# Decoder layer, mixer stage: the acausal half of the decay factors zeroed by GpSimd after the exponential instead of masked by a product before it

## What is computed

```python
def step(carry, inp):
    sr, si, px = carry
    dt_t, A_t, tr_t, th, bt, ct, xt = inp
    alpha = jnp.exp(A_t * dt_t)[:, :, None, None]
    beta = ((1.0 - tr_t) * dt_t)[:, :, None, None] * alpha
    gamma = (tr_t * dt_t)[:, :, None, None]
    base = bt[:, None, None, :] * (px[..., None] * beta + xt[..., None] * gamma)
    ...
    y = ...   # the state read out with ct
```

## Time and profile before

| what | us |
|---|---|
| median of the timed runs (3) | 699.77 (695.93 to 700.83) |
| the profiled execution, its own time | 701.77 |
| its span, first to last instruction | 700.0 |
| PE busy in the span | 610.4 (87%) |
| DVE busy | 495.2 (71%) |
| POOL busy | 261.2 (37%) |
| ACT busy | 256.6 (37%) |

### The profile page before, as it was taken

One profiled execution on the slowest core, in us unless ns is written; L12 is line 12 of the kernel. 1 busy time (PEld: TensorE's weight loads), 2 busy tenths in 40 slices (PEclk: granted clock), 3 DMA queues, 4 the chain that ended last, 5 costly groups with the idle time before them and its releaser, 6 DMA issues. The chain is left out here.

```text
span 700.0 us, 17981 instructions
## 1 busy us (share of the span) xinstructions
PE 610.4 (87%) x6368; PEld 502.8 (72%) x6368; DVE 495.2 (71%) x1246; ACT 256.6 (37%) x444; POOL 261.2 (37%) x301
## 2 busy tenths in 40 slices
PE   6589999999999754888779879779799999999995
PEld 5467778778777553676667767557688888888884
DVE  2877887887887554657567667486578778787873
ACT  2443442443343200635445435335322323332221
POOL 4263754754752575405145144362101101110111
PEclk9989999999999975789999999999999999999998
DMA  6020000000000485275484763800001000000000
GB/s 204 0 62 1 16 15 0 15 15 14 1 16 1 114 200 99 70 142 133 106 159 126 138 132 93 188 6 6 32 0 32 30 0 30 30 0 30 16 16 16
DMA packets 53553, 40.34 MB, mean 58 GB/s; under 512 B 3968, under 2 KB 48288, under 8 KB 53488
## 3 DMA queue, kind: packets, MB, share of 16 engines
q1 hardware_dynamic: 50896, 36.74, 22.2%
q0 software_dynamic: 704, 1.92, 1.2%
q10 hardware_dynamic: 1888, 0.79, 0.6%
HBM read 24.10 MB, written 11.93 MB: 51 GB/s over the span
## 5 line engine op out<-in xcount | busy, mean ns | idle before, releaser
L1917 PE MATMUL bank<-xT_hl_c,w_up 128*128 128x512 f32 x432 | 118.1, 409 | 2.4 <-ACTq L67 2.4
L1244 DVE TENSOR_REDUCE nmax<-bank 128x4 f32<-128x512 f32 x112 | 72.0, 685 | 54.9 <-PE bank L1399 48.3
L141 POOL TENSOR_TENSOR rstd<-mv,norm_c 128x4 f32<-128x4 f32 x24 | 6.4, 267 | 264.3 <-DVE mv L135 251.2
L1151 ACT ACTIVATE prob<-bank 128x512 f32<-128x512 f32 x128 | 69.4, 594 | 67.2 <-PE bank L1399 42.0
L1917 PEld LDWEIGHTS bank<-xT_hl_c,w_up 128*128 128x128 f32 x432 | 76.1, 189 | 15.9 <-ACTq L67 2.7
L1389 PE MATMUL bank<-neg_i,mask 64*128 64x256 bf16 x512 | 54.3, 292 | 36.4 <-issue 9.5
L1839 ACT ACTIVATE sg<-bank 128x512 f32<-128x512 f32 x72 | 43.0, 597 | 105.3 <-PE bank L1917 105.3
L1933 PEld LDWEIGHTS bank<-w_down,hid 128*128 128x128 f32 x576 | 74.4, 191 | 5.9 <-issue 0.5
L738 POOL TENSOR_TENSOR ramp<-upto,dec_hl 128x512 fp32r<-128x512 f32 x64 | 66.8, 1073 | 26.1 <-PE bank L866 26.1
L1933 PE MATMUL bank<-w_down,hid 128*128 128x128 f32 x576 | 75.6, 275 | 0.0
L1872 DVE TENSOR_TENSOR gu<-sg,bank 128x512 f32<-128x512 f32 x64 | 43.8, 685 | 21.5 <-PE bank L1917 10.5
(11 more groups left out here) (227 smaller groups left out, 1265.1 us busy)
## 6 DMA issues: line engine op xcount, KB each, us to landing
q_stack<-q_scratch SPq DMA_DIRECT2D x32, 192.0 KB, 5.4
k_scratch<-k_part SPq DMA_DIRECT2D x8, 384.0 KB, 3.2
q_scratch<-q_part SPq DMA_DIRECT2D x8, 384.0 KB, 2.7
k_stack<-k_scratch SPq DMA_DIRECT2D x32, 96.0 KB
x<-xT_in SPq DMA_DIRECT2D x8, 256.0 KB, 8.3
mask<-mask_in SPq DMA_DIRECT2D x8, 256.0 KB, 6.0
xres<-x_in SPq DMA_DIRECT2D x8, 256.0 KB, 2.8
q_scratch<-q_part SPq DMA_DIRECT2D x8, 256.0 KB, 3.1
```

The lines of the kernel that those rows point to most:

```text
L1151: act.activation(prob[:, b % 2, ORDER[n], :, :], (TT0, TT1)[n % 2][:, :], ACT.Exp, scale=XD ** -0.5)\
L1244: dve.tensor_reduce(nmax[:, b, 4 * u:4 * u + 4], (SS0, SS1)[n % 2][:, :].rearrange("p (i k) -> p i k", i=4), AX_X, ALU.max, negate=True).t ...
L1917: mm = pe.matmul(bank[:, :], w_up[:, which, a, c, :], xT_hl[par][:, v, :], start=(n == 0), stop=(n == 2))
```

## The change

In `front`, the product `ident` x `acausal` is gone, and `acausal` with the two POOL instructions that made it. `expo` now holds finite values in its acausal half after the exponential (all exponents are sums of decays, at most 0). A new POOL helper `causal(g, b)` waits for the exponential, and sets the entries with s > t of `expo` to 0 in place, with one affine selection over 128x512. DVE's `mix` waits for that selection instead of for the exponential. POOL's ramps and selections take turns, one ramp pair and one selection at a time; `steps_of` and `normalise_pool` stay behind them, and in group 7 the three `part_third` are spread among them.

```diff
--- before.py
+++ after.py
@@ -312,7 +312,6 @@
         w_out = t["w_out"]
         upto = sb("upto", [P, P])
         after = sb("after", [P, P], F32R)
-        acausal = sb("acausal", [P, P], BF16)
         phase = sb("phase", [P, 1])
 
         soft = sb("soft", [P, NSEQ, 2 * HEADS])
@@ -348,6 +347,8 @@
         s_xx = sem("x_mm", GS)
         s_g = sem("g_mm", GS)
         s_exp = sem("expo_ready", GS)
+        s_causal = sem("expo_causal", GS)
+        pool_passed = ctx.enter_context(nc.semaphore("mixer_pool_passed"))
         s_w = sem("w_ready", 3 * GS)
         s_mix = sem("mix_ready", GS)
         s_y = sem("y_mm", GS)
@@ -511,11 +512,6 @@
                                    pattern=[[1, P]], channel_multiplier=-1).then_inc(s_pool, 1)
                 for k, value in enumerate((LN_EPS, -0.5)):
                     pool.memset(norm_c[:, k, :], value).then_inc(s_pool, 1)
-                pool.wait_ge(s_pool, 5)
-                pool.memset(scratch[:, :], 0.0).then_inc(s_pool, 1)
-                pool.wait_ge(s_pool, 8)
-                pool.affine_select(out=acausal[:, :], in_=scratch[:, :], compare_op=ALU.is_ge, fill=NEG, base=0,
-                                   pattern=[[1, P]], channel_multiplier=-1).then_inc(s_pool, 1)
                 pool.memset(c_rot[:, :, :, :, :], 0.0).then_inc(s_off, 1)
                 pool.wait_ge(s_dve, DONE[0])
                 steps_of(pool, 0)
@@ -728,7 +724,7 @@
 
         @block.gpsimd
         def _(pool):
-            for s in (s_x1, *a.third):
+            for s in (s_x1, s_causal, *a.third):
                 s.prime(pool)
 
             def ramps(g, bs):
@@ -739,17 +735,34 @@
                                            bc(dec_hl[:, v, bass.ds(g * GS + b, 1), :].rearrange("p o h -> p (o h)")[:, :, None],
                                               [P, HEADS, P]), ALU.mult).then_inc(s_ramp.sem, 1)
 
+            def causal(g, b):
+
+                pool.wait_ge(s_exp.sem, s_exp.at(g, b))
+                pool.sem_inc(pool_passed, 1)
+                pool.affine_select(out=expo[:, b % 2, :, :], in_=expo[:, b % 2, :, :], compare_op=ALU.is_ge, fill=0.0, base=0,
+                                   pattern=[[0, HEADS], [1, P]], channel_multiplier=-1).then_inc(s_causal.sem, 1)
+
             def group(g, par, left):
-                ramps(g, (2, 3))
-                if left:
-                    ramps(g + 1, (0, 1))
+                ramps(g, (2,))
+                causal(g, 1)
+                if not left:
+                    part_third(pool, a, 0, 1)
+                ramps(g, (3,))
+                causal(g, 2)
+                if left:
+                    ramps(g + 1, (0,))
+                else:
+                    part_third(pool, a, 0, 0)
+                causal(g, 3)
+                if left:
+                    ramps(g + 1, (1,))
+                    causal(g + 1, 0)
                 if left == 2:
                     steps_of(pool, g + 2)
                 if left:
                     normalise_pool(pool, g, s_res, s_x1, res, mv, rstd, norm_c, x1[:, bass.ds(g * GS, GS), :])
                 if not left:
-                    for group_, which in ((0, 1), (0, 0), (1, 1)):
-                        part_third(pool, a, group_, which)
+                    part_third(pool, a, 1, 1)
                 if left == 1:
                     pool.memset(a.first[1][:, :, :].bitcast(F32), TWO_ONES).then_inc(a.ones, 1)
 
@@ -757,6 +770,7 @@
             ramps(0, (0, 1))
             betas(pool, 1)
             steps_of(pool, 1)
+            causal(0, 0)
             pairs(pool, group)
 
         @block.vector
@@ -807,7 +821,7 @@
                     if b:
                         inputs_of(g, b)
                     dve.wait_ge(s_g.sem, s_g.at(g, b))
-                    dve.wait_ge(s_exp.sem, s_exp.at(g, b))
+                    dve.wait_ge(s_causal.sem, s_causal.at(g, b))
                     dve.wait_ge(s_y.sem, s_y.at(g, b - 2))
                     dve.tensor_tensor(mix[:, b % 2, :, :], PG[:, :].rearrange("p (h t) -> p h t", h=HEADS),
                                       expo[:, b % 2, :, :], ALU.mult).then_inc(s_mix.sem, 1)
@@ -862,9 +876,8 @@
                 pe.wait_ge(s_ramp.sem, s_ramp.at(g, 2 * b + 1))
                 pe.wait_ge(s_exp.sem, s_exp.at(g, b - 1))
                 for v in range(2):
-                    pe.matmul(PD[:, :], after[:, :], ramp[:, b % 2, v, :, :], start=(v == 0), stop=False)
-                pe.matmul(PD[:, :], ident[:, :], bc(acausal[:, None, :], [P, HEADS, P]), start=False, stop=True)\
-                    .then_inc(s_dec.sem, 1)
+                    mm = pe.matmul(PD[:, :], after[:, :], ramp[:, b % 2, v, :, :], start=(v == 0), stop=(v == 1))
+                mm.then_inc(s_dec.sem, 1)
                 pe.wait_ge(s_w.sem, s_w.at(g, 3 * b - 2))
                 tokens(par, b, 0)
```

## The result

The changed kernel took 709.29 us (median of 4 runs, 708.48 to 713.90), the kernel before 700.30 us (4 runs). The ratio is 1.0144, with a 95% interval of 1.0086 to 1.0202. Over all runs of the study the medians are 709.2 us (7 runs) and 700.2 us (37). One run of the changed kernel, 719.5 us, was in a slower state of the chip and is left out. The profiled execution of the changed kernel took 708.48 us, with a span of 706.7.

The account below looks back on a forecast made before the run. PE was taken to bound the mixer, busy 22.25 of 23 us. The terms -6.1, +16.9, -5.2, +1.5 and +7.0 (clock) sum to +14.1 us, on a median of 699.8 us: 713.9 us, range 704 to 720.

Parts of the forecast that it names:

- the second rival: Mixer: PE stalls before theta come, but the clock stays up; 706.9 us, chance 0.26.
- The product that goes: PE in groups 0 to 6: 29 products of ident and acausal fall away at 0.21 us each, -6.1 us.
- The selection: POOL: one 128x512 selection takes 0.67 us, bounds 0.60 and 0.88.
- The stall: Start of groups 1 to 6: PE waits before theta for POOL's late steps, 6 x 2.81 = +16.9 us.
- What the stall covers: Groups 1 to 6: PE's waits for ramps and `mix` vanish behind the stall, -5.2 us; late `rotate` costs nothing.
- The end of the mixer: Group 7: two selections ahead of the third part of q delay SP's stores, +1.5 us.
- The clock: PE behind the stalls: granted clock falls to 0.50 after five of six, 5 x 1.4 = +7.0 us.
- The third: Mixer: DVE becomes late as well, `w_tok` held 0.57 us in each of six groups, +3.4 us; 717.3 us, chance 0.12.
- The fourth rival: Mixer: POOL finishes selection and steps before PE reaches theta, and `rotate` isn't late; 690.0 us, chance 0.06.

Follow-up runs that it names:

- busy_stall: The changed kernel with ten more 128x512 matmuls of PE ahead of each wait for the steps, their result overwritten by theta: 704.6 us.
- product_back: The changed kernel with the product of ident and acausal kept as well: 711.7 us.
- after_again: The changed kernel, unchanged, profiled and measured again: 709.2 us.
- q_part_early: The changed kernel with, in group 7 alone, the third part of q ahead of the selection of sequence 2: 709.4 us.
- two_selections: The changed kernel with the selection of the next group's sequence 0 done twice over: 713.7 us.
- both_early: The changed kernel with POOL's steps and ramps of the next group's sequence 2 ahead of its sequence 0's selection and the normalisation, group 6's memset also earlier: 688.7 us.
- steps_first: The changed kernel with the steps for theta made ahead of the selection of the next group's sequence 0: 701.9 us.

## Why the prediction was right, and which terms were off

The direction, the mechanism and its place were right, and 709.3 us lies in the range. The size was 9 us, not 14. The total alone wouldn't have told the forecast from the second rival, whose 706.9 us lies nearer to 709.3 than 713.9 does; the six stalls and the four falls of the clock in the trace do. Term by term, for the point where the attention begins (12.0 us instead of 14.1):

- **The product that goes**, -6.1 us. Taken out of the kernel before it was worth about 5.2 us (4.23 in six groups, and group 0). The difference is the one product per group that only lengthens a wait for ramps.
- **The selection**, 0.67 us on a line between two sizes: 0.64 us undisturbed, 0.70 us in the mean.
- **The stall**, 6 x 2.81 = 16.9 us: from output to theta 2.61, 2.66, 2.63, 2.64, 2.60 and 2.44 us more than before, 15.6 us. Every link of the chain was there.
- **What the stall covers**, -5.2 us: together with the 24 products of groups 1 to 6 the sum had 10.2 us. Without falls of the clock (busy_stall) theta to output was 9.0 us shorter. The remaining 1.2 us are put down to `rotate` and `mix`, which come late by more than the stall covers: in busy_stall's trace PE's weight loads wait for `rotate` six times, 2.7 us in all. The prediction called that gap "some tenths" and priced it at nothing.
- **The end of the mixer**, +1.5 us: 2.2 us. The part of q ends 1.85 us later after the first ramp, behind two selections of 0.64 and 0.82 us and a ramp pair that took 2.49 us instead of 2.02. Why the second selection and the ramps took longer was not tested.
- **The clock**, 5 x 1.4 = 7.0 us: the term that was most off. It fell four times, at 1.1 us each, 4.4 us. That the fall follows such a stall was right, and theta itself did lose 1.5 us. But PE, when slow, later waits less for `rotate`, and gets some of it back: such waits are two in the changed kernel (1.0 us), six in busy_stall (2.7 us). Where the product keeps PE busier (product_back), the two falls cost 1.65 and 1.39 us (24.19 and 23.93 us from theta to output against 22.54), so there the prediction's 1.4 was right. The rule "nearly as long, so five of six" had no more behind it than one row. Stalls of the same 2.3 to 2.5 us were followed by a fall four times in six (changed, after_again), twice (product_back) and five times (q_part_early); the stalls of 2.9 to 3.2 us of two_selections, six times in six. In the changed kernel a stall of 2.46 us was not followed by a fall, the next one of 2.48 us was (PEclk is the third number from the end):

```profile
125.20:128.70 3.50, 3.44 (x23) 3.17 (x24) 2.35 (x6) 1.38 (x2) 3.10 (x4) 1.00 0.23 68
152.00:155.50 3.50, 3.50 (x18) 3.46 (x18) 2.48 (x3) 0.72 (x2) 3.23 (x4) 0.52 0.19 56
```

- **The attention** was counted as unchanged. It took 238 to 251 us in the profiles of this study. The other 3 us lie there; whether by chance or through the change stayed open.

Of the rivals, the second (no fall of the clock) is what busy_stall makes: its attention begins 10.1 us later than before, 7.6 us without the 2.5 of group 0's products, against the 7.1 us of the sum without the clock. The third was right that DVE becomes slower, though it named `w_tok`, and most of it fell on `frac`. In group 2 of the changed kernel, on DVE and POOL, and then all `frac` products in the kernel before, the changed one and both_early (ns min/median/max):

```profile
103.04 2.57 DVE L398 TENSOR_TENSOR frac<-ang,whole 128x512 f32<-128x512 f32 x2
...
103.97 1.09 POOL L742 TENSOR_SCALAR_AFFINE_SELECT expo<-expo 128x512 f32<-128x512 f32 x1
105.03 2.69 POOL L734 TENSOR_TENSOR ramp<-upto,dec_hl 128x512 fp32r<-128x512 f32 x2
...
L397 DVE TENSOR_TENSOR frac<-ang,whole x16: 677/678/1524, 31.8 to 202.2; 128x512 f32<-128x512 f32 x16
...
L398 DVE TENSOR_TENSOR frac<-ang,whole x16: 682/1121/1527, 30.5 to 213.6; 128x512 f32<-128x512 f32 x16
...
L398 DVE TENSOR_TENSOR frac<-ang,whole x16: 677/679/1526, 30.7 to 195.4; 128x512 f32<-128x512 f32 x16
```

The selection, made while `frac` ran, took 1.09 us instead of 0.64, and `frac` in the median 1.12 instead of 0.68. The Trainium skill (SBUF — State Buffer, Who interferes with whom) says that a DVE instruction with two SBUF inputs and a GpSimd instruction that reads SBUF exclude each other for their whole length. These rows agree with it, in both directions. both_early makes the selections at other times, and `frac` is back at 0.68 us there (`w_tok` is at 0.68 in the median, against 0.43 before), so which DVE operation is slow goes with the time of POOL's work. What it costs on the path no run takes apart; it is at most the 1.2 us above and what the end of the mixer lost beyond the prediction. The fourth rival, faster, would have needed the mid-group selections hidden too; steps_first and both_early show that this takes another order of POOL's program.

## What to carry to other kernels

An engine with idle time isn't free for work that has to wait: what stands behind the wait in its program moves to the end of that wait. So before work goes to a "half idle" engine, ask of each new wait when it ends, and who needs the next instruction behind it. Put the instructions that nobody holds up (here the steps and the ramps of sequence 2) ahead of those that wait; here that order alone was worth 9 us, and the mask's move from PE to POOL nothing on top of it. And compare milestones inside the stage that was changed, since another stage may vary by more than the change is worth.

## What was unexpected of the hardware

Ten extra 128x512 products in each stall made groups 1 to 6 of the mixer 4.8 us shorter, 4.4 us of it because the granted clock then stayed at 1.00. The clock cost 1.1 us per fall in the changed kernel and not the 1.5 us by which theta's own products were longer, but 1.4 to 1.65 us with the product back. Stalls of equal length were followed by a fall in some groups and not in others, even in the same kernel, and behind two longer ones the clock stayed low for 6.8 us instead of 3.4. And the attention, untouched, took 250.7 us in one execution and 238.4 in another of the same kernel, at a mean granted clock of 0.88 and 0.93.
